# A two-layer graph network on one core: layer 0's finishing of a pair spread over three groups, x in two buffers

## What is computed

```python
# layer 0
t1 = x @ W1
msg = (t1[src] + (x[src] * x[dst]) @ W2) / (sqrt(deg[src]) * sqrt(deg[dst]))[:, None]
embed = leaky_relu(where(in_cnt > 0, t1 + segment_sum(msg, dst), 0) + b, 0.01)
x = layernorm(x + embed / maximum(norm(embed, axis=1), 1e-12))
# layer 1
xt = x @ W.T + b
x = layernorm(x + segment_sum(xt[src], dst) / (in_cnt + 1))
```

## Time and profile before

| | |
|---|---|
| median of 3 runs | 3845.7 us |
| the three runs | 3844.35, 3845.70, 3852.46 us |
| the profiled execution's own time | 3845.26 us |
| its span, first to last instruction | 3843.5 us |
| preparation, before the first L709 gather | 371.5 us |
| layer 0, round 0 to the first gather of layer 1 | 371.5 to 1938.7 us |
| layer 1 | 1938.7 to 3843.5 us |
| busy: POOL, PE, DVE, ACT | 2894.7, 2707.4, 1930.4, 497.7 us |

### The profile page before, as it was taken

How to read it: one execution, slowest core, us unless ns; L and a number is a source line. 1 busy time by engine, 2 the same in 40 slices (tenths; PEclk the granted TensorE clock), 3 DMA queues, 4 the chain that set the end, 5 groups by cost and what they waited for, 6 DMA issues and landing times.

```text
span 3843.5 us, 66285 instructions
## 1 busy us (share of the span) xinstructions
PE 2707.4 (70%) x10342; PEld 1851.4 (48%) x10342; DVE 1930.4 (50%) x3848; ACT 497.7 (13%) x1540; POOL 2894.7 (75%) x3055
## 2 busy tenths in 40 slices
PE   4552777777767666667777777777777777777776
PEld 3442556555555555656644443434444444344443
DVE  8996566666666566666642333333333333333333
ACT  8992000000000000000000000000000000000000
POOL 7777777777777777777777777777777777777776
PEclk5555888888888888888877777877787877777777
DMA  7879455555555555555444444444444444444443
GB/s 254 274 237 337 151 164 166 163 165 164 164 164 165 164 164 164 165 164 163 146 125 122 129 126 129 125 131 124 132 125 130 125 127 127 129 127 130 126 127 113
DMA packets 327431, 598.55 MB, mean 156 GB/s; under 512 B 72589, under 2 KB 211394, under 8 KB 327074
## 3 DMA queue, kind: packets, MB, share of 16 engines
q0 software_dynamic: 145680, 398.00, 36.4%
q1 hardware_dynamic: 153528, 174.96, 13.8%
q10 hardware_dynamic: 27866, 22.52, 1.9%
HBM read 507.24 MB, written 76.03 MB: 152 GB/s over the span
## 4 chain that ended last, share of the span: by engine, by line
POOL 32%; SPq 23%; issue 22%; ACTq 9%; DMA 6%; ACT 5%; PE 2%; DVE 1%; DVEq 0%; POOLq 0%
POOL ring L709 32%; SPq L517 16%; ACT dst_rel L797 4%; ACTq L907 4%; SPq L510 4%; DMA ring<-x,idx 3%; PE banks L1603 2%; ACTq L818 1%; ACTq L932 1%; ACTq L884 1%; DMA ring<-src_lo 1%; DMA src_lo<-scaled_x 1%; SPq L438 1%; SPq L433 1%; SPq L491 1%
## 5 line engine op out<-in xcount | busy, mean ns | idle before, releaser
L1603 PE MATMUL banks<-ring,hot_space 128*128 128x257 f32 x6252 | 2095.9, 472 | 567.3 <-DMA ring<-x,idx 464.8
L1603 PEld LDWEIGHTS banks<-ring,hot_space 128*128 128x128 f32 x6252 | 1274.8, 226 | 1319.3 <-DMA ring<-x,idx 946.5
L709 POOL DMA_INDIRECT ring<-x,idx x1506 | 1426.7, 947 | 461.9 <-issue 451.9
L709 POOL DMA_INDIRECT ring<-scaled_x,idx x1241 | 1188.7, 958 | 381.0 <-issue 372.1
L1272 DVE SCALAR_TENSOR_TENSOR big<-banks,here_mask,big 128x257 f32 x784 | 343.2, 479 | 1342.9 <-PE banks L1603 1328.1
L1174 DVE TENSOR_TENSOR hot_space<-banks,dst_rel 128x1024 f32<-128x1024 f32 x344 | 421.0, 1225 | 175.7 <-issue 174.2
L1534 PE MATMUL banks<-ident,halves 128*128 128x128 f32 x588 | 136.2, 392 | 370.3 <-DVE halves L1286 368.5
L720 POOL DMA_INDIRECT ring<-in_x,src_col x276 | 263.9, 956 | 84.3 <-issue 83.8
L1534 PEld LDWEIGHTS banks<-ident,halves 128*128 128x128 f32 x588 | 105.3, 204 | 408.4 <-DVE halves L1286 363.7
L797 ACT ACTIVATE dst_rel<-columns,halves 128x128 bf16<-128x128 f32 x960 | 268.3, 377 | 5.3 <-DVE halves L1087 5.3
L836 ACT COPY idx<-src_col 128x32 int32 (+1 forms) x97 | 21.1, 218 | 1827.9 <-issue 915.0
(11 more groups left out here) (149 smaller groups left out, 1241.2 us busy)
## 6 DMA issues: line engine op xcount, KB each, us to landing
src_lo<-x ACTq DMA_DIRECT2D x3648, 1.0 KB
src_lo<-x SPq DMA_DIRECT2D x3648, 1.0 KB
src_lo<-scaled_x SPq DMA_DIRECT2D x2944, 1.0 KB
kept_rows<-ring SPq DMA_DIRECT2D x94, 384.0 KB, 3.2
ring<-kept_rows SPq DMA_DIRECT2D x47, 768.0 KB
ring<-x,idx POOLq DMA_INDIRECT x1506
src_lo<-scaled_x ACTq DMA_DIRECT2D x1408, 1.0 KB
ring<-scaled_x,idx POOLq DMA_INDIRECT x1241
```

Of the source, the lines that this page charges most:

```text
L709: g.indirect_dma_start(ring[:, u, 0:D], None, rows, bass.IndirectOffsetOnAxis(ap=idx[:, idx_buf(layer, n), u:u + 1], axis=0)).then_inc(row ...
L1603: last = nc.tensor.matmul(group_sum(k % SUMS), dst_hot[:, k % HOTS, u - k * GT, :], ring[:, u, 0:DW], start=u == tiles[0], stop=u == tiles ...
```

## The change

- x gets two buffers of two tiles each (`x_space`), used by even and odd pairs. Both tiles of a pair count on one semaphore.
- In layer 0, SP issues the next pair's x between the two hand parts of a round, and waits there for the moments of one pair earlier. It stores the pair of two rounds ago, and not of one, at the round's end.
- In layer 0, DVE makes the squares in group 0 as before, but the moments only in group 1 behind the `mix`, and normalizes in group 2. ACT's second root stands behind `clear_sums`, in front of the copies of the transposed halves. Round 48 keeps the old arrangement.
- In layer 1 DVE's order is the same, and x is loaded one pair earlier relative to the moments. DVE's loop body now has two rounds in place of one, in both layers.
- The small tiles `base_row` and `base_row_f` of the preparation lie in `out_t`.

```diff
-        x_t = [sb(f"x_t{n}", [P, D]) for n in range(2)]
+        x_space = sb("x_space", [P, 4, D])
+        x_t = [[x_space[:, 2 * n + s, :] for s in range(2)] for n in range(2)]
...
-        x_now = [x_t[n][:, :] for n in range(2)]
+        x_now = x_t[0]
...
+        def x_count(layer, buf, turn):
+
+            return 32 * (layer * (ROUNDS // 2 + 1 - buf) + turn + 1)
...
-            def next_x(layer, m):
-
-                sp.wait_ge(var_ready, node_no(layer, m) + 1)
+            def next_x(layer, m, buf):
+
+                if layer or not (isinstance(m, int) and m == 0):
+                    sp.wait_ge(var_ready, node_no(layer, m))
                 for s in range(2):
-                    load_x(layer, m + 1, 2 * m + 2 + s, s)
+                    load_x(layer, m + 1, 2 * m + 2 + s, s, buf)
...
                     hand_part(layer, hand, 2 * half)
+                if layer == 0:
+                    next_x(layer, i - 1, buf)
+                if hand is not None:
                     hand_part(layer, hand, 2 * half + 1, load_next)
                 if extra is not None:
                     extra_part(*extra)
-                next_pair(layer, i - 1)
+                if layer == 1:
+                    next_x(layer, i - 1, buf)
+                    store_pair(layer, i - 1)
+                elif not (isinstance(i, int) and i == 1):
+                    store_pair(layer, i - 2)
...
-                if ended:
+                if ended and (layer or last):
                     roots(layer, i - 2)
+                elif ended:
+                    norm_root(i - 2)
...
                 if sums and layer == 0 and not last:
                     clear_sums(i - 1)
+                    if ended:
+                        var_root(layer, i - 2)
...
-            def mix(m, sums, xs=x_now, mask=pair[0], last=False):
+            def mix(m, sums, arrived, xs=x_now, mask=pair[0], last=False):
...
+                v.wait_ge(*arrived)
                 for s in range(2):
-                    v.wait_ge(x_in[s], 16 * (m + 1))
...
                     if ended and k == 0:
-                        finish_sums(layer, i - 2, acc[:, bass.ds(2 * i - 4, 2), :])
-                        moments(layer, i - 2)
-                    if ended and k == LAST_K and not last:
+                        finish_sums(layer, i - 2, acc[:, bass.ds(2 * i - 4, 2), :], x_arrived(layer, buf, turn - 1), x_t[buf])
+                        if whole:
+                            moments(layer, i - 2, x_t[buf])
+                    if ended and k == LAST_K and layer == 1 and not last:
                         norm(layer, i - 2)
                     if sums and k == LAST_K and layer == 0:
-                        mix(i - 1, acc[:, bass.ds(2 * i - 2, 2), :])
+                        mix(i - 1, acc[:, bass.ds(2 * i - 2, 2), :], x_arrived(0, 1 - buf, turn - 1 + buf), x_t[1 - buf])
+                        if ended and not last:
+                            moments(layer, i - 2, x_t[buf])
+                    if ended and k == LAST_K + 1 and not whole:
+                        norm(layer, i - 2)
...
-                    with v.Fori(2, KEPT_ROUNDS) as i:
-                        round_(layer, i, True, True, layer == 0)
+                    with v.Fori(1, KEPT_ROUNDS // 2) as h:
+                        for n in range(2):
+                            round_(layer, 2 * h + n, n, h, True, True, layer == 0)
```

More of the change, by code:

```diff
@@ L447, in load_x_last, with store_pair, one_pair @@
                 rows = table[1] if layer else x
-                for n in range(2):
-                    sp.wait_ge(x_in[n], 16 * (node_no(layer, ENDS - 1) + 1))
+                sp.wait_ge(x_in[0], x_count(layer, 0, ENDS // 2 - 1))
                 sp.dma_start(x_last[0], rows[first:first + P, :]).then_inc(x_in[0], 16)
-                sp.dma_start(x_last[1][0:LAST_ROWS, :], rows[first + P:NODES, :]).then_inc(x_in[1], 16)
-            def next_x(layer, m):
+                sp.dma_start(x_last[1][0:LAST_ROWS, :], rows[first + P:NODES, :]).then_inc(x_in[0], 16)
+            def next_x(layer, m, buf):
+                if layer or not (isinstance(m, int) and m == 0):
+                    sp.wait_ge(var_ready, node_no(layer, m))
+                for s in range(2):
+                    load_x(layer, m + 1, 2 * m + 2 + s, s, buf)
+            def store_pair(layer, m):
+                for s in range(2):
+                    store(layer, m, 2 * m + s, s)
+            def one_pair(layer, m):
                 sp.wait_ge(var_ready, node_no(layer, m) + 1)
@@ L457, in next_x @@
                     load_x(layer, m + 1, 2 * m + 2 + s, s)
-            def store_pair(layer, m):
-                for s in range(2):
-                    store(layer, m, 2 * m + s, s)
-            def next_pair(layer, m, last=False):
-                if last:
-                    sp.wait_ge(var_ready, node_no(layer, m) + 1)
-                else:
-                    next_x(layer, m)
                 store_pair(layer, m)
@@ L561, in pass_extra, with middle_round @@
                 sp.dma_start(ring[:, EXTRA_U, 0:D], extra_rows.bitcast(F32)).then_inc(extra_over, 16)
-            def middle_round(layer, i, kept_ahead=False, places_ahead=False, hand=None, half=0, load_next=False, extra=None):
+            def middle_round(layer, i, kept_ahead=False, places_ahead=False, hand=None, half=0, load_next=False, extra=None,
+                             buf=0):
                 if kept_ahead:
@@ L610, in _ @@
                         middle_round(layer, 2, hand=2, half=0)
-                        middle_round(layer, 3, hand=2, half=1, load_next=True, extra=(1, 0))
+                        middle_round(layer, 3, hand=2, half=1, load_next=True, extra=(1, 0), buf=1)
                         pass_hand(layer, 2)
@@ L614, in _ @@
                             middle_round(layer, SPAN * g, hand=2 * g + 1, half=0, extra=(g, 1))
-                            middle_round(layer, SPAN * g + 1, hand=2 * g + 1, half=1, load_next=True, extra=(g, 2))
+                            middle_round(layer, SPAN * g + 1, hand=2 * g + 1, half=1, load_next=True, extra=(g, 2), buf=1)
                             pass_hand(layer, 2 * g + 1)
@@ L631, in _ @@
                         sp.sem_inc(table1_whole, 1)
-                    next_pair(layer, ROUNDS - 2, last=True)
+                    store_pair(layer, ENDS - 1)
                     if layer == 0:
@@ L1262, in _, with x_arrived @@
             nc.vector.memset(ring[:, :, D:DW], 1.0).then_inc(ring_ones, 1)
+            def x_arrived(layer, buf, turn):
+                return x_in[buf], x_count(layer, buf, turn)
             def load_block(i, k):
@@ L1288, in mix, with finish_sums @@
                 ordered()
[L1290 removed]
+            def finish_sums(layer, m, sums, arrived, xs=x_now, mask=scal, results=project, rows=out_now):
                 if rows is out_now:
@@ L1356, in norm, with round_ @@
                 ordered()
-            def round_(layer, i, sums, ended, find=False, last=False):
+            def round_(layer, i, buf, turn, sums, ended, find=False, last=False):
+                whole = layer or last
                 block = load_block(i, 0)
```

64 lines of the change are left out of this document (33 added, 31 removed).

## The result

The changed kernel takes 3867.4 us, the median of 5 runs (3862.6 to 3867.5), and the kernel before 3846.6 us on the same chip, median of 5 runs (3844.4 to 3852.5): 20.8 us more. The ratio is 1.0049, with a 95% interval of 1.0038 to 1.0060. The forecast was 3845.5 us, "same" at 88%. The profiled execution took 3865.1 us with a span of 3863.0 us, 19.5 us over the span before.

A forecast was written before the change was run, and what follows sets the result against it. POOL, issuing gathers back to back, was taken as the bound: 371.5 + 3455.5 + 16.5 = 3843.5 us of span, every part of the change costing 0, hence 3845.5 us as forecast time, range 3838 to 3853 us.

The forecast's parts named there:

- the first and the last term of the sum: On POOL: 371.5 us before the first of the L709 gathers, and a tail of 16.5 us after the last.
- (4): SP's new wait on var_ready amid the hand rows asks for moments one pair older, so it costs 0.
- (1): x earlier on SP: mix's 3.0 us wait a round goes, SP's lap stays about 32.2 us, gain 0.
- (2): Moments and norm behind mix on DVE: mix 7.5 us earlier, PE's 9.7 us wait shrinks to some 2, gain 0.
- (3): ACT's second root before the copies: copies net earlier by 4 us, cost 0, POOL's 2.6 us margin should grow.
- (5): The change of layers: POOL's 2.6 us wait stays; up to 2.3 us could go, taken as 0.
- (6): Loop bodies of two rounds and out_t in the preparation: no POOL instruction differs, cost 0 in both outer terms.
- rival "slower": Index copies on ACT in layer 0 come too late for POOL; 0.5 us a round gives 3866 us; chance 6%.
- 47 d - 2.6: POOL's loss in us if a round of ACT and SP became d longer, past the 2.6 us margin.
- open term: Layer 0 gathers take 958 ns against 947, 13.7 us in all; taken as 0 with 3 us either way.

The follow-up runs named there:

- e2: The changed kernel with SP's x loads and their wait behind both halves of the hand rows, store still late: 3858.2 us, ratio 1.0013.
- e6: The changed kernel with only the x loads moved behind the second half of the hand rows, the wait on the moments left between the halves: 3865.1 us, ratio 1.0045.
- e9: The changed kernel with SP's store of the pair two back moved up to the x loads, between the halves of the hand rows: 3863.4 us, ratio 1.0047.
- e1: The changed kernel, but in layer 0 the squares write to the projection's PSUM bank and only the moments wait for the store: 3855.8 us, ratio 1.0006.
- e7: The changed kernel with only its part on x; moments, normalizing, roots and store placed as in the kernel before: 3849.7 us, ratio 1.0006.
- e11: The kernel before with 8 increments of an idle semaphore on SP in every second round of layer 0: 3853.7 us, ratio 1.0021.
- e8: The kernel before with 16 increments of an idle semaphore on SP in every second round of layer 0: 3864.3 us, ratio 1.0042.
- e4: The kernel before with one hand-row register load written twice on SP, the second dropped when the kernel was built: 3852.7 us, ratio 0.9996.
- e10: The changed kernel with the store between the halves of the hand rows and the x loads behind the second half: 3849.9 us, ratio 1.0005.
- e3: The changed kernel with squares written apart from out_t and x loads behind both halves of the hand rows: 3857.4 us, ratio 1.0008.
- e12: The changed kernel with x loads behind the second half of the hand rows, plus 16 increments on SP every second round of layer 0: 3858.8 us, ratio 1.0032.

## Why the prediction was wrong

The bound was read right. POOL alone sets the time, its gathers kept their 947 and 958 ns, and the first and the last term of the sum did not move. The scale of the risk was there too: "the margins shrink because the loop of the other engines is a little slower than POOL", with 2.6 us left.

**The step that failed is (4)**, SP's new wait: "it asks for moments one pair older than before, so it costs 0". The pair is older, but the change also moves the store a round later, and the squares write the tile that is being stored. The wait for that store was never in the sum. Through it the moments of the older pair hang on a store that SP itself issues behind its wait. The loop is 30.5 us long in the round shown and closes on SP in every second round. e2 and e6 show its price: with the wait behind the hand rows the kernel is 4.6 us over the kernel before, and POOL does not stand; with the wait between them it is 18.5 us over.

**Step (1) failed with it**: "the loads, stores and hand rows are as many as before, so SP's lap stays about 32.2 us". They were as many; the waits were not. The `x` loads had covered the landing of the last hand rows, which the prediction did not cost when it moved them. Added up over SP's steps in 24 rounds, two rounds grew by 1.6 us: 1.5 us at the pass of the hand rows, 0.5 us at the loads of `x`, 0.4 us in issuing hand rows, and 0.5 us less at the loop's end, with 0.3 us of waits before that are gone. The two waits trade with each other: e6 keeps the lap with most of the landing covered, e9 with the loop open. So neither alone is the 1.6 us.

**Steps (2) and (3)** had the order right and the time wrong. `mix` no longer waits for `x`, as (1) said. But it did not come 7.5 us earlier: the squares, which stand in front of it on DVE, now wait 9 us in each round. PE's wait for `halves` should have shrunk to 2 us a round and grew to 11:

```profile
PE banks L1564 <- DVE halves L1308: 264.2, 24, 13.8
...
ACT scal L878 <- DVEq L1070: 188.4, 24, 11.9
```

The first answers to the 243.1 us in the earlier trace rows. ACT stands 7.9 us a round in front of its first root with half of its hand rows and the next index copy queued behind. Step (3) counted what is queued behind the second root only, and gave "POOL's margin should grow". The lag grew by 10.7 us and the margin went. Its "net earlier by 4 us" was not seen in any run: with the squares freed of the store (e1) the lag is 21.7 us, no shorter than the 21.2 before, though the moments still wait 2.3 us a round for the store there. The margin did grow in e1, to 14.9 us in round 41, but because SP was 9 us ahead at its 40th kept load. That e7's lag is 4.7 us shorter does not bear (3) out, since e7 has the moments and the roots where the kernel before has them.

**Steps (5) and (6)** held: the change of layers cost 3.0 us instead of 2.6, the first gather starts at 371.1 us and the tail is 16.2 us.

**The rival "slower"** named the place (the index copy on ACT), the margin of 2.6 us, and a time of 3866 us for 0.5 us a round. It got 6% because its cause was sought in the moments ahead of the copies; it was the store, two queues away. Its formula, 47 d - 2.6, stands up to the doses: e11 has d = 0.21 us and cost 6.6 us (formula 7.5), e8 d = 0.51 us and 17.8 us (formula 21). For the changed kernel d is 0.79 us and the formula gives 34 us where 20.8 were measured. Two terms are missing in it: the 17.6 us by which SP starts the layer earlier, and the 10.7 us of lag. With both, up to the 40th kept load, the copy is 28.3 - 17.6 + 10.7 = 21.4 us later; less the 1.6 us of margin that could be used up (2.6 before, 1.0 is none) that is 19.8 us, about what POOL lost.

**The open term**, the 11 ns by which a gather is longer in layer 0, is untouched by the change: 958 ns still. The `x` loads were pulled out of SP's burst of transfers, and the gathers did not gain, which speaks against bursts of that size. The Trainium skill, SBUF — State Buffer, section "Who interferes with whom", would have the time with DVE's two-input instructions, of which there are as many as before; so far the trace agrees. No run tests it: in e1 only the output of the squares goes to PSUM, both their inputs are in SBUF as before, and the gathers took 960 ns there as against 961 in e4, the kernel before on the same chip. It was not settled here.

**What stays open.** The landing of the last hand rows takes 2.9 us from the last issue in the changed kernel, and 1.6 to 2.0 us in e1, e7, e9 and e10; what makes it longer was not found. In e9 and e10 the four register loads of SP in two rounds take 9.3 and 8.9 us instead of 8.4 to 8.6, and the cause isn't known. The kernels without stalls (e1 to e3, e10) are 2 to 5 us slower than the kernel before, with gathers of 960 to 965 ns in layer 0; but e4, the kernel before once more, has 961 ns as well, so this is not shown to be the reason. The difference is at the edge of what can be measured, and no version beat the kernel before.

## What to carry to other kernels

When a step is moved a round later, list the buffers that it releases as well as those that it needs: here the store moved with the normalizing, and the next user of `out_t` stood 10 us ahead of it. When a wait is moved to the middle of an engine's queue, follow what it waits for back until the chain ends or comes back to the same queue; if it comes back, the loop's length has to be compared with the round. A margin that shrinks round by round is a sum of small differences over 47 rounds, so "the engine is off the critical path" holds only while its lap is unchanged: measure the price of 1 us on it (here 18 us for 1 us in each two rounds) before touching its order.

## What the runs showed of the hardware

An increment on SP costs 0.06 us (e8: 16 of them 0.95 us in two rounds), cheap enough to be used as a dose. Where SP waited for it, the landing of a block of 1 KB hand rows came 1.6 us (e9) to 3.6 us (e12) after the last issue, as a mean of each kernel. A second, identical register load disappears when the kernel is built (e4: 229 as before), so extra work put in as a price has to have an effect of its own.
